# A written-out expert stage with fixed first tiles, and input loads cut into small pieces

## The reference

```python
def xattn(query, key, value):                      # d=128, 16 heads, window of 64: the whole sequence
    Q, K, V = query @ Wq.T + bq, key @ Wk.T + bk, value @ Wv.T + bv     # split into heads
    attn = softmax(Q @ K.T / sqrt(8))
    return (attn @ V) @ Wo.T + bo

def ffn(x):
    h = layernorm(x) * gamma + beta
    q = lambda W: clip(round(W / s), -1, 1) * s    # s: mean of |W| over the last axis
    shared = silu(h @ q(shared_w1).T) @ q(shared_w2).T
    probs = softmax(h @ router_w.T); e = argmax(probs)
    return shared + max(probs) * (silu(h @ q(expert_w1[e]).T) @ q(expert_w2[e]).T)

x = x + xattn(layernorm(x), ctx, ctx)
x = x + ffn(layernorm(x))
```

## Time and profile before

| | |
|---|---|
| median of 3 runs | 306.35 us (306.12 to 310.66) |
| the profiled execution | 306.09 us, of which span 304.3 |
| turns | to about 208 us |
| table, first loads, first h | 208 to 224 us |
| steps | 224 to about 298 us |
| PE busy | 250.2 us (82%) |
| DVE, ACT, POOL busy | 206.4, 165.8, 133.2 us |
| granted TensorE clock, mean | 0.886 |
| DMA | 37.04 MB, mean 122 GB/s |

### The profile page before, as it was taken

One profiled execution on the slowest core, in us unless ns is written; L12 is line 12 of the kernel. 1 busy time (PEld: TensorE's weight loads), 2 busy tenths in 40 slices (PEclk: granted clock), 3 DMA queues, 4 the chain that ended last, 5 costly groups with the idle time before them and its releaser, 6 DMA issues.

```text
span 304.3 us, 10486 instructions
## 1 busy us (share of the span) xinstructions
PE 250.2 (82%) x3407; PEld 211.0 (69%) x3408; DVE 206.4 (68%) x782; ACT 165.8 (54%) x412; POOL 133.2 (44%) x209
## 2 busy tenths in 40 slices
PE   7778999799999999999999999741069797898950
PEld 5556777688888777977888777621059686797940
DVE  7683789479889889689898698647225456364530
ACT  2452677178577586486675655310068676686720
POOL 8691023064355246246344443554003465466571
PEclk9675899599999999799999999955559999999995
DMA  6598989525635554454555600101233344244100
GB/s 214 175 246 219 336 242 248 136 74 123 154 110 129 119 149 100 104 147 104 120 146 153 144 21 20 37 35 71 51 91 100 106 109 130 71 121 132 48 34 0
DMA packets 65007, 37.04 MB, mean 122 GB/s; under 512 B 37294, under 2 KB 60082, under 8 KB 64704
## 3 DMA queue, kind: packets, MB, share of 16 engines
q1 hardware_dynamic: 62144, 30.07, 38.4%
q0 software_dynamic: 2816, 6.37, 5.8%
HBM read 20.60 MB, written 16.33 MB: 121 GB/s over the span
## 4 chain that ended last, share of the span: by engine, by line
PE 61%; DVE 13%; issue 8%; SPq 7%; DMA 3%; POOL 3%; ACT 1%; POOLq 0%; DVEq 0%; ACTq 0%
PE bank L848 10%; PE bank L647 8%; PE bank L610 5%; PE bank L829 4%; PE bank L630 3%; PE bank L634 3%; PE bank L834 3%; PE bank L584 3%; DMA k_t<-qk_terms 3%; PE bank L597 3%; PE bank L589 2%; SPq L384 2%; PE bank L678 2%; PE bank L664 2%; PE bank L671 2%
## 5 line engine op out<-in xcount | busy, mean ns | idle before, releaser
L561 POOL DMA_INDIRECT out<-o_rows,o_idx x40 | 39.3, 983 | 47.3 <-DVE o_idx L1376 39.6
L931 ACT ACTIVATE e_t<-bank,lne 128x512 f32<-128x512 f32 x64 | 42.1, 683 | 25.6 <-PE bank L634 25.5
L1091 DVE TENSOR_REDUCE negmax<-bank 128x8 bf16<-128x512 f32 x64 | 42.0, 685 | 7.2 <-PE bank L610 6.6
L533 POOL DMA_INDIRECT rows_by_expert<-rows,dest x32 | 32.4, 1012 | 19.8 <-POOL rows L521 13.8
L848 PE MATMUL bank<-t,g 128*128 128x128 f32 (+1 forms) x320 | 39.9, 279 | 0.0
L647 PE MATMUL bank<-v_t,e_t 128*64 128x18 f32 x1024 | 35.6, 212 | 2.3 <-ACT e_t L931 1.8
L848 PEld LDWEIGHTS bank<-t,g 128*128 128x128 f32 x320 | 37.3, 192 | 0.0
L647 PEld LDWEIGHTS bank<-v_t,e_t 128*64 128x64 f32 x1024 | 32.6, 138 | 4.7 <-ACT e_t L931 2.6
L630 PE MATMUL bank<-negmaxT,sel 128*128 128x128 bf16 x256 | 35.7, 225 | 0.0
L634 PE MATMUL bank<-q_t,k_t 128*128 128x64 f16 x512 | 35.7, 196 | 0.0
L634 PEld LDWEIGHTS bank<-q_t,k_t 128*128 128x128 f16 x512 | 32.5, 100 | 2.1 <-issue 0.3
(11 more groups left out here) (163 smaller groups left out, 582.9 us busy)
## 6 DMA issues: line engine op xcount, KB each, us to landing
qk_terms<-qk_hl SPq DMA_DIRECT2D x64, 128.0 KB, 2.3
in_rows<-rows_by_expert SPq DMA_DIRECT2D x40, 130.0 KB
q_t<-qk_terms SPq DMA_DIRECT2D x16, 256.0 KB
k_t<-qk_terms SPq DMA_DIRECT2D x64, 64.0 KB
w_in<-in_ffn SPq DMA_DIRECT2D x3, 768.0 KB, 6.1
rows_by_expert<-zeros SPq DMA_DIRECT2D x8, 130.0 KB, 2.8
x_all<-in_x SPq DMA_DIRECT2D x1, 1024.0 KB, 8.4
c_t<-in_ctx SPq DMA_DIRECT2D x1, 1024.0 KB, 9.5
```

The lines of the kernel that those rows point to most:

```text
L533: nc.gpsimd.indirect_dma_start(by_expert, bass.IndirectOffsetOnAxis(ap=dest[:, r, i:i + 1], axis=0), rows[:, r, i, :], None).then_inc(scat ...
L561: nc.gpsimd.indirect_dma_start(out, bass.IndirectOffsetOnAxis(ap=o_idx[:, r, i:i + 1], axis=0), o_rows[:, r, i, :], None, bounds_check=TOK ...
L931: fn(e_t[:, i, hh].rearrange("p a b c -> p (a b c)"), ST[hh][:, :], ACT.Exp, bias=lne_col, scale=SCALE).then_inc(e_done[hh], 1)
L1091: v.tensor_reduce(negmax[:, i, 8 * hh:8 * hh + 8], A[hh][:, :].rearrange("p (a b) -> p a b", b=S), X, ALU.max, negate=True).then_inc(max_d ...
```

## The change

- `GROUPS` has seven groups in place of four: chunks 8 to 15 of x and context come in pairs of chunks, 256 KB a load, behind `load_terms` of turns 1, 3, 5 and 7. Before, all of them came in turn 0, ahead of its stores.
- Weight blocks 3 to 8 are loaded one by one (256 KB), block 3 before turn 0, the others behind `load_terms` of turns 2, 4, 6, 8 and 10. `clear_regions` is behind turn 0's `load_terms`.
- Turns 16 and 17 have an order of their own on PE, ACT, DVE and POOL. The last chunk's attention and projection use the score banks. The counts are summed from `seen` and the last chunk's one-hot rows, so POOL's last `add_seen` is gone.
- Slots 0 to 7 are tile 0 of each expert, without the table; the table holds the 31 slots of later tiles. There are 39 slots in place of 40; the last of the 20 steps has one tile. SP, PE and ACT wait for the table at step 4. DVE still works it out before its first split.
- All steps are written out, with constant addresses except for the table's values. PE does `layer1(0)` ahead of `turn_h(1)`, and loads the experts' numbers ahead of `turn_h`. ACT loads the Silu table by a small instruction before the steps.

```diff
-    SLOTS = -(-((TOKENS + EXPERTS * (TILE - 1)) // TILE) // 8) * 8
-    STEPS = SLOTS // 2
+    LATER_SLOTS = NT - 1
+    SLOTS = EXPERTS + LATER_SLOTS
+    STEPS = -(-SLOTS // 2)
+    FIXED = EXPERTS // 2
...
-        GROUPS = ((0, 1), (1, 4), (4, 8), (8, NCH))
+        GROUPS = ((0, 1), (1, 4), (4, 8), (8, 10), (10, 12), (12, 14), (14, NCH))
...
-            for u in range(4):
-                body(u, u % ROWBUFS, u)
-            with eng.Fori(4, STEPS - 4 - (ROWBUFS - 1), ROWBUFS) as u:
-                for j in range(ROWBUFS):
-                    body(u + j, (4 + j) % ROWBUFS, 4 + j)
-            for u in range(STEPS - 4, STEPS):
-                body(u, u % ROWBUFS, u)
+        def tiles(u):
+            return range(min(2, SLOTS - 2 * u))
+
+        def landed(u):
+            return sum(16 * len(tiles(w)) for w in range(u % 2, u + 1, 2))
+
+        def steps(body):
+            for u in range(STEPS):
+                body(u, u % ROWBUFS, u % 2)
...
-            load_ffn_weights(1)
+            load_ffn_weights(3, 1)
...
             def body(c, r, k):
-                if k == 0:
-                    load_x(3)
-                    load_c(3)
-                if k == 1:
-                    clear_regions()
-                    load_ffn_weights(2)
                 if has(k + 3):
                     store_terms(c + 3, 0)
                     store_terms(c + 3, 1)
...
                     load_terms(c + 2)
+                if k == 0:
+                    clear_regions()
+                if k in (1, 3, 5, 7):
+                    load_x(3 + k // 2)
+                    load_c(3 + k // 2)
+                if k in (2, 4, 6, 8, 10):
+                    load_ffn_weights(3 + k // 2, 1)
...
-            sp.wait_ge(tab_done, 1)
             sp.wait_ge(scattered[0], NCH * 16)
             sp.wait_ge(scattered[1], NCH * 16)
...
+                if u == FIXED:
+                    sp.wait_ge(tab_done, 1)
+                for i in tiles(u):
+                    if u < FIXED:
+                        row = (2 * u + i) * TOKENS
+                        rows_of = by_expert[row:row + TILE]
+                    else:
+                        k = 2 * (u - FIXED) + i
+                        row = sp.value_load(tab[0:1, 0, k:k + 1], min_val=0, max_val=EXPERTS * TOKENS - TILE)
+                        rows_of = by_expert[bass.ds(row, TILE), :]
+                    sp.dma_start(in_rows[:, m, i, :], rows_of).then_inc(rows_loaded[r], 16)
...
-                if has(k - 2):
+                if has(k - 2) and k < NCH + 1:
                     add_seen(c - 2, k - 2)
...
+                if k == NCH:
+                    attend(c * 2 - 1, 1 - r, 1)
+                    turn_n2(c - 2, r, lambda: pe.wait_ge(attnT_ready, c - 1))
+                    for hh in range(2):
+                        pe.wait_ge(e_done[hh], NT)
+                    turn_attn(c - 1, 1 - r, nothing)
+                    route(c - 2, lambda: pe.wait_ge(dest_done, c - 2))
+                    proj_o(c - 1, nothing)
+                    count(c - 2, k, lambda: pe.wait_ge(shifted_done, c - 1))
+                    return
+                if k == NCH + 1:
+                    turn_n2(c - 2, r, lambda: pe.wait_ge(hT_ready, c - 2))
+                    route(c - 2, lambda: pe.wait_ge(dest_done, c - 2))
+                    pe.wait_ge(x2_done, c - 2)
+                    count(c - 2, k, lambda: pe.wait_ge(shifted_done, c - 1))
+                    for n, some in enumerate((seen[:, :], onehot_b[:, 0, :], onehot_b[:, 1, :])):
+                        last = mm(M0[:, 0:EXPERTS], ones_b[:, :], some, start=(n == 0), stop=(n == 2))
+                    last.then_inc(counts_done, 1)
+                    return
...
-                if k + 1 < STEPS:
-                    turn_h(u + 1, (m + 1) % ROWBUFS, k + 1)
-                if k in (4, STEPS - 4):
-                    loaded[1 - r] = experts_of(u - 1)
                 loaded[r] = experts_of(u)
-                layer1(u, r, k, loaded[r])
-                if k >= 1:
-                    layer2(u - 1, 1 - r, k - 1, loaded[1 - r])
+                if u == 0:
+                    layer1(u, r, loaded[r])
+                if u + 1 < STEPS:
+                    turn_h(u + 1, (m + 1) % ROWBUFS, 1 - r)
+                if u >= 1:
+                    layer1(u, r, loaded[r])
+                    layer2(u - 1, 1 - r, loaded[1 - r])
...
+            fn(warm[:, :], lne[:, :], ACT.Silu)
+            keep_h(0, 0)
+            steps(body)
...
+            v.tensor_scalar(valid[:, 0:EXPERTS], cnt[:, :], part_no[:, 0:1], None, ALU.is_gt)
```

More of the change, by code:

```diff
@@ L434, in body @@
                 carry_waits(sp)
-                for i in range(2):
-                    row = sp.value_load(tab[0:1, 0, bass.ds(u * 2 + i, 1)], min_val=0, max_val=EXPERTS * TOKENS - TILE)
-                    sp.dma_start(in_rows[:, m, i, :], by_expert[bass.ds(row, TILE), :]).then_inc(rows_loaded[m % 2], 16)
-            steps(sp, body)
-            for r in range(2):
-                sp.wait_ge(out_stored[r], STEPS * 16)
+                if u == FIXED:
[10 more added lines that the diff above has]
+            steps(body)
+            for u in (STEPS - 2, STEPS - 1):
+                sp.wait_ge(out_stored[u % 2], landed(u))
         @block.gpsimd
@@ L565, in _ @@
             pool.sem_inc(rows_free, ROWBUFS)
-            steps(pool, store_rows)
+            steps(store_rows)
         @block.tensor
@@ L981, in body @@
                     keep_negmaxT(c * 2 + 1, 1, k)
-                if has(k - 1):
+                if has(k - 1) and k < NCH:
                     keep_attnT(c - 1)
@@ L1015, in silus, with body @@
                         last = fn(g32[:, r, 1, c, i * TILE:(i + 1) * TILE], F1[r][1][:, c * CH + i * TILE:c * CH + (i + 1) * TILE],
-                                  ACT.Silu, scale=s1[:, bass.ds(e * 2 + (2 + c), 1)])
+                                  ACT.Silu, scale=scale_of(e, c))
                 last.then_inc(g32_done, 1)
-            def body(u, m, k):
-                r = m % 2
-                experts = [act.value_load(tab[0:1, 1, bass.ds(u * 2 + i, 1)], min_val=0, max_val=EXPERTS - 1) for i in range(2)]
-                if k + 1 < STEPS:
-                    keep_h(u + 1, 1 - r, k + 1)
-                silus(u, r, k, experts)
-            act.wait_ge(tab_done, 1)
-            keep_h(0, 0, 0)
-            steps(act, body)
+            def body(u, m, r):
+                experts = experts_of(u)
+                if u + 1 < STEPS:
+                    keep_h(u + 1, 1 - r)
+                silus(u, r, experts)
+            fn(warm[:, :], lne[:, :], ACT.Silu)
+            keep_h(0, 0)
+            steps(body)
         @block.vector
@@ L1355, in split_h, with finish_rows @@
                 dve.wait_ge(h_chain, u + 1)
[L1356 to L1360 removed]
+                v.tensor_tensor(h_lo[:, r, 0:w], h32[:, r, 0:w], h_hi[:, r, 0:w], ALU.subtract).then_inc(h_done, 1)
+            def finish_rows(u, m, r):
+                w = len(tiles(u))
                 dve.wait_ge(f2_done, u + 1)
[L1362 to L1363 removed]
+                dve.wait_ge(rows_loaded[r], landed(u))
+                if u >= 1:
@@ L1364, in finish_rows @@
                     dve.wait_ge(parts_done, u)
-                for i in range(2):
-                    v.scalar_tensor_tensor(o_part[:, i, :], YY[r][:, (2 + i) * D:(3 + i) * D], in_rows[:, m, i, GATE:GATE + 1],
-                                           in_rows[:, m, i, D:2 * D], ALU.mult, ALU.add).then_inc(part_done, 1)
-                v.scalar_tensor_tensor(o_idx_f[:, :], in_rows[:, m, :, TOKEN], -NOWHERE, valid[:, bass.ds(u * 2, 2)],
+                for i in tiles(u):
+                    last = v.scalar_tensor_tensor(o_part[:, i, :], YY[r][:, (2 + i) * D:(3 + i) * D], in_rows[:, m, i, GATE:GATE + 1],
+                                                  in_rows[:, m, i, D:2 * D], ALU.mult, ALU.add)
```

234 lines of the change are left out of this document (140 added, 94 removed).

## The result

| | kernel before | changed kernel |
|---|---|---|
| median of runs | 308.13 us of 4 (306.12 to 310.66) | 287.06 us of 4 (283.18 to 299.65) |
| ratio, 95% interval | | 0.922 (0.906 to 0.938) |
| forecast | | 288.0 us, as a ratio to 306.35: 0.940 |
| second measurement | 308.61 of 11 | 288.31 of 7, ratio 0.926 (0.917 to 0.934) |

The medians are of all runs, while the ratios leave out every run more than 1.5% above the quickest of its kernel. The changed kernel's microseconds agree with the forecast, the gain does not. The kernel before turned out at 308 in the median where 306.35 had been shown, and the changed kernel gained what the sum had and something more.

A forecast was written before the change was run, and what follows sets the result against it. Bound by a chain of waits, 61% on PE, with losses in turn 2, the last two turns, the steps' start and the expert steps. 306.09 - 4.1 - 4.0 - 8.7 - 1.3 = 288.0 us, range 284.5 to 296.5.

The forecast's parts named there:

- the loads' term: Turns 0 to 10: reordered loads end turn 2's stall and the low clock after it, -4.1 us, bounds 0 and -4.1.
- rival 1: Turn 2 stays long because the eight clears still stand ahead of the terms: 292.1 us, chance 0.15.
- Steps: Expert steps: written out, all 20 take the written-out pace of 2.94 us, -8.7 us from step 0 to 15.
- Start: Start of expert steps: SP and PE no longer wait for the table, -4.0 us including the last turns' 0.6.
- Last turns: Last two turns: the output projection follows the router at once, -0.6 us, between +0.5 and -1.2.
- Store: End of the kernel: the 40th tile's store is gone, -1.3 us.
- Small loads behind the terms: Turns 1 to 8 and 10: loads added behind the terms are covered by slack and cost nothing.
- the rival at 316.7: Small loads hold up the terms, seven turns each losing 4.1 us to stall and low clock: 316.7 us, chance 0.03.
- Late code: Expert steps: written-out code is fetched late, four stalls of at most 2.9 us each, 299.6 us, chance 0.04.

The follow-up runs named there:

- old_loads: The changed kernel with the load order of the kernel before: 294.22 us, ratio 0.958; run again on a fifth chip, 322.98 us, ratio 0.963.
- loads_only: The kernel before with only the changed kernel's load order: 304.48 us against 308.61, no interval.
- steps_only: The kernel before with all 20 expert steps written out, 40 slots, all from the table: 300.13 us, ratio 0.978.
- changed, first: Profile of the unaltered changed kernel from the first measurement: profiled run 299.65 us, span 297.8 us.
- clears_later: The changed kernel with the eight clears behind the terms of turn 1 instead of turn 0: 286.6 us, ratio 0.934.
- table_wait: The changed kernel, but SP waits for the table ahead of its first load, as in the kernel before: 287.94 us, ratio 0.935.
- old_turn16: The changed kernel with turn 16 in its old order: 288.58 us, ratio 0.940.
- after_fourth: The changed kernel, unaltered, on the fourth chip, one of the slower kind: 321.77 us, no interval.
- loop_steps: The changed kernel with steps 6 to 17 as a hardware loop of two passes of six, on the fourth chip: 325.65 us, no interval.
- before_again: The kernel before, unaltered, on the fourth chip: 344.89 us; another copy of the same kernel took 337.02 there.
- before_third: The kernel before, unaltered, on the fifth chip: 340.65 us, ratio 1.015.
- after_third: The changed kernel, unaltered, on the third chip, one of the slower kind: 326.79 us, ratio 0.975.
- the one that seemed to hold the clock up: The changed kernel with half of the next scores ahead of the attention's transposes on PE: 285.26 us, ratio 0.928; on the fourth chip 330.40 us.

## Why the prediction was wrong

**The step that failed is the loads' term**: "PE needs the terms 1.74 us earlier. ... I take the stall as gone, and with it the low clock that follows it: -4.1 us", with "0 ... and -4.1" as bounds. The loads did gain time, but the stall was not gone, and the term was too small.

The size. On the chip of the second measurement `old_loads` has everything but the loads. The sum had 14.0 us for that, and it came: 14.4 by the medians, 13.0 by the ratio. The loads took the rest, 5.9 or 9.9 us in place of 4.1. Against this stands `loads_only` with 4.1 in the other kernel, so their worth is not settled more closely.

What the term had wrong is its measure. It took the stall of 1.74 us for all the time to be won ahead of the low clock. In the pair of the result the terms are there 3.21 us earlier (54.90 and 51.69), but PE too is sooner at turn 2, by 2.97, so 1.51 us of stall are left; from there to turn 3 it takes 6.46 us at a clock of 0.56 and 3.84 at 1.00, 2.62 less. And 1.74 us is the smallest of the six sums of waits in the old order. The clock tells why. The stretch of 20 to 30 us, first of before, then of steps_only (columns as above):

```profile
20.00:30.00 10.00, 8.26 (x49) 6.75 (x48) 5.24 (x20) 3.62 (x10) 3.30 (x2) 0.50 0.92 229
```

```profile
20.00:30.00 10.00, 9.98 (x121) 8.05 (x119) 7.37 (x24) 6.30 (x15) 3.39 (x3) 0.86 0.91 217
```

At 0.50 PE reached the scores late, and little was left to wait. At 0.86 it is there sooner and waits longer, 3.59 us in turn 1 and 1.54 in turn 2 (steps_only; L605 is the scores' line):

```profile
42.42 1.07 PE L605 MATMUL bank<-k_t,q_t 128*64 128x256 f16 x8 [3.59 <-DMA k_t<-qk_terms]
...
55.08 0.63 PE L605 MATMUL bank<-k_t,q_t 128*64 128x256 f16 x8 [1.54 <-DMA k_t<-qk_terms]
```

In the old order the arrival of the terms sets where turn 3 starts, not before 58.1 in six profiles, whatever PE gains; in the new one it can start at 52.1. So the lower bound of -4.1, turn 2 at turn 4's length, was none: the new order also frees what the old one took back from a lucky start, up to 6.0 us between the two earliest.

The mechanism: the stall did not always go. In three of eight profiles, all on ordinary chips, PE still waits 1.4 to 1.5 us. Ahead of the terms stand the clears, as rival 1 ("The eight clears alone are 4.6 us of SP's time ahead of the terms, and they stay") said; in changed, first, the chain of waits (36 to 52 us) has eight pieces of L418 from 37.70 to 43.24, and the stores of chunk 4 only behind them.

```profile
37.70 1.40 SPq L418
...
41.60 1.17 SPq L418
...
42.81 0.43 SPq L418
...
43.38 0.38 SPq L384
```

In the changed kernel's profiles these eight hold SP for 5.15 and 5.54 us, where 4.62 had been read before. That they make the rest of the stall fits `clears_later`, which has none, but is not shown, as said there. Rival 1's price, all of turn 2's excess, was wrong, as the clock did not fall behind a stall of 1.5 us in the changed kernel and its repeat; in `table_wait` turn 2 did stay at 15.19.

By `old_loads` the loads' term is short by 1.8 us of the 2.2 missing there by the medians, and by 5.8 of 4.8 by the ratios. Where all of it falls stays open: on ordinary chips only 4.3 us lie ahead of turn 3, and on the slower chips turn 3 starts 7.7 us sooner with no gain that the times show. The rest is no more than the spread of a program whose runs range over 16 us; the shown 306.35 itself was 1.1 to 2.3 under the later medians (307.4 to 308.6) of the same kernel. That 287.06 us came out so near 288.0 is luck: the kernel before had been shown some 2 us quicker than its later medians, and the change gained some 2 to 3 us more than the sum.

**Steps: right in pace, a microsecond short.** -8.7 forecast, -7.68 between steps 0 and 15 here, the difference being step 0 to 1, 3.97 instead of 2.94, at a granted clock of 0.64 from 219.0 to 222.2 us (the first second layer took 3.03). `steps_only` has -8.5 by the medians, -6.9 by the ratio and -6.0 in its profile. **Start: right, underestimated by 1.1** for two reasons: my 6.0 us from the first layer to the second was 5.42 (213.71 to 219.13), and SP issued 5.03 us behind `dest`, where 213.0 less 207.3 (`dest` of the earlier trace rows less 0.6), so 5.7, had been taken. The two terms meet at step 0's second layer, and their sum fits to 0.1. **Last turns**: 0.3 in the pair and 0.4 against `old_turn16`, of the 0.6. **Store**: right. **Small loads behind the terms: at nothing, right**: turns 3 to 10 show no `k_t` wait and the rival at 316.7 appeared nowhere. Ten added transfers did not add up to 20 us either: `x_all` loads of 256 KB take 3.8 us to land in changed, but the next load, of `c_t`, is issued 0.66 us behind (48.53 and 49.19). The Trainium skill ("DMA: Bandwidth & Descriptors", Anatomy of one DMA) has some 2 us of each transfer fixed, in a fit for those that GpSimd issues; these are SP's.

**Late code** had 0.04 and four stalls of 2.9 us. On the ordinary chips no profile of written-out steps has one; behind the first step, which falls into the low clock, the longest are 4.25 us in `steps_only` and 4.24 in `clears_later` (15 to 16), and they go with waits for a store and for `in_rows`. On the three other chips PE stops for nothing recorded, in smaller and more pauses, and in all kernels. The Trainium skill ("Runtime: NRT & Kernel Launch", Instruction fetch mechanics) has instructions fetched in blocks, with crossing one "mostly hidden". The trace has DMA packets of the kind `instruction`, which I take for the fetches of code. In the steps of after_fourth (234 to 306 us) there are

```profile
q8 instruction: 5, 0.08, 0.4%
q14 instruction: 6, 0.05, 0.2%
```

(queue, kind: packets, MB, share of 16 engines), and in those of changed (219 to 284 us) also 5 and 6. So the slower chip fetches no more often, and its 16 pauses are more than the packets; of loop_steps' pauses four lie between 271 and 307 us, in the second pass, where the trace has two such packets of 8 KB and none of the larger ones. That speaks against late code as the cause; a fetch that is late unrecorded is not excluded, and what these chips do differently stays open. What is measured is that the gain shrinks: from `dest` to the end of the span 107.0 and 108.0 us before (before_again, before_third) against 98.9 and 99.7 changed (after_third, after_fourth), so some 8 us instead of 13.65.

## What to carry to other kernels

When an engine waits for a transfer, the wait that one profile shows is what the engine's own start left over; cost the removal by when the data arrive, not by the idle time, and look at a second profile before calling the idle time a bound. Terms that the profile shows at both ends, such as a loop's pace against the written-out pace or an extra store, summed to 0.3 us over the 96 us behind `dest`, though single ones were off by up to 1.1. A variant that looks better in one profile is to be run again beside the original, on another chip if possible: the one that seemed to hold the clock up was 8.6 us slower the next time. And means over profiles are to be kept apart by kind of chip: here one mean of 5.4 us stood for 4.3 and 7.7.

## What was not expected of the hardware

**The clock falls by execution, not by code.** On ordinary chips turns 4, 6, 8 and 10, which have a weight block, last 11.25 us, or 12.75 to 12.9, or 14.0 to 14.3 (the last in the changed kernel and its variants alone). By estimate such turns make most of the spread of runs, four times 3.0 us in changed, first, which has 299.65 us and a mean clock of 0.861, the three unprofiled runs beside it 0.898, 0.920 and 0.927 at 289.00, 285.13 and 283.18. Two profiles of the same kernel in turn 4, changed, first,

```profile
72.00:73.00 1.00, 1.00 (x18) 0.95 (x17) 1.00 (x3) 0.62 (x2) 0.92 (x2) 1.00 0.89 332
73.00:74.00 1.00, 0.93 (x29) 0.76 (x25) 0.93 (x4) 0.25 (x2) 0.88 (x2) 1.00 0.99 306
74.00:75.00 1.00, 0.56 (x6) 0.43 (x8) 0.89 (x6) 0.37 (x2) 0.20 (x1) 1.00 0.33 96
75.00:76.00 1.00, 1.00 (x14) 0.62 (x11) 1.00 (x4) 1.00 (x3) 0.02 (x1) 0.53 0.49 133
```

and changed:

```profile
70.60:71.60 1.00, 1.00 (x20) 0.95 (x20) 1.00 (x3) 0.53 (x2) 0.90 (x3) 1.00 0.75 273
71.60:72.60 1.00, 0.85 (x25) 0.68 (x21) 0.93 (x4) 0.33 (x2) 0.84 (x2) 1.00 0.96 272
72.60:73.60 1.00, 0.63 (x8) 0.49 (x10) 0.89 (x6) 0.34 (x2) 0.20 (x1) 1.00 0.08 19
73.60:74.60 1.00, 1.00 (x16) 0.75 (x11) 1.00 (x4) 0.96 (x3) 0.20 (x1) 1.00 0.72 203
```

PE's busy time is nearly the same, with one pause of 0.50 or 0.52 us before the attention's transposes; the granted clock fell in the one and stayed in the other.

**Three of the chips are 9% slower** (the kernel before at 337 instead of 308), while single operations off PE take nearly what they take elsewhere: the exponentials 683 ns in before and changed, 683 and 684 in before_again and after_fourth; a store on POOL 983 ns in the first two and 1003 and 1001 in the others. PE pauses more, as shown above, and its mean granted clock is lower, 0.853 and 0.851 in before_again and before_third against 0.886 in before; which of the two comes first no run here tells.
